# An adaLN attention and ternary feed-forward kernel on one core: weight preparation of the first attention spread anew over VectorE, GpSimd and ScalarE

## The chip, the core and the metric

The kernel runs on one core of a Trainium2 chip. The metric is the device time of one execution in microseconds (us). Engines are named as in the profile: PE is TensorE, PEld its weight load, DVE is VectorE, ACT is ScalarE, POOL is GpSimd, SP is SyncE, whose queue issues DMAs. PSUM banks have the names QA, QB, T, F0, F1, SA, SB, PV; the profile prints F0 and F1 both as F.

## What is computed

For each of 16 sequences of 256 tokens and 512 features, an adaptive RMS norm, an attention of 16 heads, an output projection, and a feed-forward part with ternary weights; the input is added at the end.

```python
xn = rms_norm(x, g_norm) * (1.0 + scale) + shift          # scale, shift = emb @ W_emb + b_emb
q, k, v = split(xn @ W_qkv)                               # 16 heads of 32
q, k = rms_norm(q, g_q), rms_norm(k, g_k)
o = softmax(q @ k.T * 32 ** -0.5) @ v
y = o + o @ W_out
def ternarize_weights(w):
    gamma = mean(abs(w))
    return sign(round(w / (gamma + EPS))) * gamma
h = gelu(bitlinear(y, w_fc))                              # bitlinear: layer norm, then x_hat @ ternary(w).T
x = x + bitlinear(h, w_proj)                              # w_fc 2048x512, w_proj 512x2048
```

## The kernel before

The kernel is written engine by engine; the order of each engine's instructions is fixed by hand, and semaphores tie the engines together. It runs as a pipeline over sequences: `iteration(i)` works on up to five sequences at once (`late` = i-2 second feed-forward half, `ffn` = i-1, `att` = i, `qkv` = i+1, `pre` = i+2). Each iteration has a front part (maxima of the logits, layer norm, eight feed-forward units) and then a loop `for h in range(HEADS)` over the 16 heads of `att`, in which all other work is placed by tables from head number to step.

Iteration 0 is the first with attention. No feed-forward part runs in it. In its place the weights of both feed-forward matrices are made ternary and W_out's low half is made, all between the head steps. It is the only iteration that the change touches. Its head loop runs from about 57 us to about 102 us of the trace.

One head step `h` is, on each engine:

- PE: `scores(h)` into bank SA or SB (line 892; F0 and F1 for heads 2 and 3; it waits for `p_lo` of head h-2, in heads 4 and 5 of head h-4), then the fillers (pieces of the next sequence's q, k, v projection, lines 760 to 762), then `values(h-2)` into PV (lines 907 to 909), then `column_sums(c)` where the table `COLSUM_AT` has one (line 754, waits for `s_sign`), then one use of the bank T: a `heads` transpose (line 917) or a `piece` transpose of `qkn` (line 1068). `values` of the first head of each group of four waits for `o_sb` of the group before.
- ACT: exponential (line 1209), its f16 copy `p_hi` (line 1215), then a `Square` of a finished piece (line 1227), the high half of the transposed piece or heads (lines 1251, 1280), and last a sign pass of 2048 columns where `SIGN_AT` has one (line 1126).
- DVE: in heads 5, 9 and 13 first `heads_out` (lines 1408, 1410: reads PV, writes `o_sb`), then `p_lo` (line 1557), then the low halves, sums of squares `ssq` (line 1579), `qkn` (line 1583, waits for POOL's `rqk`), and last `out_weights_lo` (line 1341), `fc_cut` (lines 1330 and 1332, a pair) and `dve_round` (line 1318).
- POOL: only the power -0.5 for `rx` (line 672) and `rqk` (line 710), each when its `ssq` has come.

The weights of one ternary matrix are four blocks of 128x2048. A block (w, k), w 0 for w_fc and 1 for w_proj, goes through these steps: rounding (multiply by `inv`, add MAGIC, in place, f32), then either ACT's sign pass or DVE's `fc_cut` into f16. ACT's sign of block (1, 0) and (1, 1) also waits for `s_fcut` 1, that of (1, 2) and (1, 3) for `s_fcut` 2, since their destination lies over the raw blocks that `fc_cut` reads. PE's `column_sums(c)` waits for the sign of (1, c).

POOL rounds blocks (0, 2), (0, 3), (0, 0) ahead of iteration 0, right behind the scaling of W_out's high half (lines 655 and 660). DVE rounds (0, 1) and all four of w_proj in the head loop. The tables that the change touches, as they stand before:

```python
WO_LOW_AT, G_K_AT = 2, 3
DVE_ROUND_AT = {1: (0, 1), 4: (1, 0), 6: (1, 1), 9: (1, 2), 10: (1, 3)}
POOL_ROUNDS = (2, 3, 0)
FC_CUT_AT = {3: 0, 5: 1}
SIGN_AT = {6: (1, 0), 8: (1, 1), 10: (1, 2), 12: (1, 3)}
COLSUM_AT = {8: 0, 10: 1, 12: 2, 14: 3}
```

At the end of iteration 0, PE transposes piece 3 (line 1068), then the last heads (line 917). With that the front part of iteration 1 starts (line 760 into SA), and SP issues the 16 `stk` transfers.

Of the kernel before, what the change touches and what calls it, by code (L numbers as in the profile page):

```python
# [9 lines left out]
ALU = mybir.AluOpType  # L10
# [62 lines left out]
FIRST_V_AT = 9  # L73
SECOND_FILLER = {2: QKV[0][0:2], 3: QKV[0][2:4], 4: QKV[1][0:2], 5: QKV[1][2:4], 6: QKV[2][0:2], 7: QKV[2][2:4],
                 9: QKV[3][0:2], 10: QKV[3][2:4], 12: V[0][0:2], 14: V[0][2:3], 15: V[0][3:4] + V[1][0:1]}
SECOND_SQUARE_AT, SECOND_NORM_AT = {3: 0, 5: 1, 8: 2, 11: 3}, {4: 0, 7: 1, 10: 2, 13: 3}
SECOND_TURN_AT = {6: ("heads", 0), 7: ("piece", 0), 9: ("piece", 1), 10: ("heads", 1), 12: ("piece", 2),
                  14: ("heads", 2), 15: ("piece", 3)}
FIRST_SQUARE_AT, FIRST_NORM_AT = {0: 0, 1: 1, 3: 2, 5: 3}, {2: 0, 4: 1, 6: 2, 9: 3}
# [11 lines left out]
               10: [("q", n) for n in range(6, 8)]}  # L91
SUMS_AFTER_LOW = 3

SCALE_AT, SECOND_SCALE_AT = {1: (0,), 2: (1,), 3: (2,), 4: (3,)}, {12: (0, 1), 13: (2, 3)}

MAGIC = 1.5 * 2.0 ** 23
WO_LOW_AT, G_K_AT = 2, 3
FC_ABS_AT = {1: 0, 3: 1, 5: 2, 7: 3}
PROJ_ABS_AT, PROJ_ABS_ORDER = {12: 0, 14: 1}, (0, 1, 3, 2)
DVE_ROUND_AT = {1: (0, 1), 4: (1, 0), 6: (1, 1), 9: (1, 2), 10: (1, 3)}  # L100
DVE_ROUNDS = [DVE_ROUND_AT[h] for h in sorted(DVE_ROUND_AT)]
POOL_ROUNDS = (2, 3, 0)
FC_CUT_AT = {3: 0, 5: 1}
SIGN_AT = {6: (1, 0), 8: (1, 1), 10: (1, 2), 12: (1, 3)}
SIGNS = [(0, 2), (0, 3)] + [SIGN_AT[h] for h in sorted(SIGN_AT)]
WQ_LOW_UNIT, WQ_LOW_AT = {0: (0, 0, KT), 2: (1, 0, KT // 2)}, {1: (1, KT // 2, KT), 2: (2, 0, KT)}
WQ_LOW_DONE = (1, 3, 4)
COLSUM_AT = {8: 0, 10: 1, 12: 2, 14: 3}


def place(h):
# [27 lines left out]
def first(b):  # L139

    return isinstance(b, int) and b == 0
# [20 lines left out]
def early(b):  # L162

    return isinstance(b, int) and b < 1
# [19 lines left out]
def rms_at(i):  # L184

    return FIRST_RMS_AT if i == -1 else SECOND_RMS_AT if i == 0 else None
# [43 lines left out]
def adaln_ffn_kernel(nc, x, xT, condT, w_emb, b_emb, g_norm, g_qk, w_qkv, w_out, w_fcT, w_projT, out):  # L230
    with ExitStack() as ctx:  # L231
        def sb(name, shape, dt=F32):
            return ctx.enter_context(nc.sbuf_tensor(name, shape, dt))
# [4 lines left out]
        def sem(name):  # L238
            return ctx.enter_context(nc.semaphore(name))
# [26 lines left out]
        inv = sb("inv", [P, 2])  # L266
# [67 lines left out]
        ffn_raw = [[proj_raw[:, 0:F], proj_raw[:, F:2 * F], hs_raw[:, F:2 * F], hg_raw[:, 0:F]],  # L334
                   [hq_raw[:, 0:F], hq_raw[:, F:2 * F], hs_raw[:, 0:F], hg_raw[:, F:2 * F]]]
# [297 lines left out]
        def _(pool):  # L633
# [13 lines left out]
            def first_weights():  # L647
# [10 lines left out]
                pool.wait_ge(s_abs, 4)  # L658
                for k in POOL_ROUNDS:
                    pool.tensor_scalar(ffn_raw[0][k], ffn_raw[0][k], inv[:, 0:1], MAGIC, ALU.mult, ALU.add  # L660
                                       ).then_inc(fc_round, 1)

            def iteration(i):
# [17 lines left out]
                def add_q(n):  # L681
                    pool.wait_ge(hsq_r, nth(ffn, UNITS, n + 1))
                    if n > 1:
                        pool.wait_ge(sumq_r, nth(ffn, UNITS - 1, n - 1))
                    pool.tensor_tensor(acc[:, 1, :], hq[:, 0, :] if n == 1 else acc[:, 1, :], hq[:, n, :], ALU.add  # L685
                                       ).then_inc(sumq_r, 1)

                if pre is not None and not early(pre) and rms_at(i) is None:
                    rms(pre)
                if ffn is not None:  # L690
# [29 lines left out]
        def _(pe):  # L720
# [85 lines left out]
            def iteration(i):  # L806
# [230 lines left out]
                for h in range(HEADS):  # L1037
# [21 lines left out]
                    if isinstance(i, int) and i == -1 and h == FIRST_V_AT:  # L1059
                        weight_sums(0)  # L1060
                    if isinstance(i, int) and i == 0 and h in COLSUM_AT:
                        column_sums(COLSUM_AT[h])
                    kind, n = turn_at(i).get(h, (None, 0))
# [39 lines left out]
        def _(act):  # L1103
# [14 lines left out]
            def signs(w, k):  # L1118

                if (w, k) in DVE_ROUNDS:  # L1120
                    act.wait_ge(s_dround, DVE_ROUNDS.index((w, k)) + 1)
                else:
                    act.wait_ge(fc_round, POOL_ROUNDS.index(k) + 1)
                if w:
                    act.wait_ge(s_fcut, k // 2 + 1)
                act.activation(ternary_rows(w, k), ffn_raw[w][k], ACT.Sign, bias=unmagic[:, 0:1]).then_inc(s_sign, 1)
# [20 lines left out]
            def iteration(i):  # L1147
# [57 lines left out]
                for h in range(HEADS):  # L1205
# [81 lines left out]
        def _(dve):  # L1287
# [33 lines left out]
            def fc_cut(k):  # L1321

                dst = ternary_rows(0, k)
                if k == 0:
                    dve.wait_ge(wo_h, 2)
                if k == 0:
                    dve.wait_ge(fc_round, POOL_ROUNDS.index(0) + 1)
                else:
                    dve.wait_ge(s_dround, DVE_ROUNDS.index((0, 1)) + 1)
                dve.tensor_scalar(dst, ffn_raw[0][k], MAGIC, 1.0, ALU.subtract, ALU.min).then_inc(s_cut, 1)  # L1330
                dve.wait_ge(s_cut, k + 1)
                dve.tensor_scalar(dst, dst, -1.0, None, ALU.max).then_inc(s_fcut, 1)
# [148 lines left out]
            def iteration(i):  # L1481
# [67 lines left out]
                for h in range(HEADS):  # L1549
# [87 lines left out]
                    if isinstance(i, int) and i == 0 and h == WO_LOW_AT:  # L1637
                        out_weights_lo()
                    if isinstance(i, int) and i == 0 and h in FC_CUT_AT:
                        fc_cut(FC_CUT_AT[h])  # L1640
                    if isinstance(i, int) and i == 0 and h in DVE_ROUND_AT:
                        dve_round(*DVE_ROUND_AT[h])
                    if isinstance(i, int) and i == 0 and h == HEADS - 1:
# [51 lines left out]
```

## Time and profile before

| | |
|---|---|
| device time, median of 3 runs | 1096.38 us (1095.32 to 1097.99) |
| the profiled execution | 1096.41 us, of which the span of the trace is 1094.5 us |
| busy share of the span | PE 96%, PEld 61%, DVE 83%, ACT 73%, POOL 50% |
| head loop of iteration 0 | about 57 to 102 us |

The profile is one execution with a start and a duration for every instruction. From 120 us on the PE is busy in nearly every slice of the profile; the only stretches with gaps on the PE are the first 120 us and the last few. The trace is read here through the order in time of one engine's instructions, the waits, and the busy time of each engine in a stretch.

### The profile page before, as it was taken

Reading aid. Unit: us, or ns where it says so; the run is one execution under the profiler, and the core shown is the slowest. Engines: PE = TensorE matmul, PEld = TensorE weight load, DVE = VectorE, ACT = ScalarE, POOL = GpSimd, SP = SyncE. Lnnn points to the kernel's source line nnn. Section 1 sums busy time; section 2 is a strip of 40 time slices with the busy share of each in tenths; the row PEclk is TensorE's granted clock in tenths of the full one; section 3 lists DMA queues with packets and bytes.
Section 4 is the critical chain, followed back from the end, with each engine's and each line's share of the span. In section 5 each row is a group of like instructions: output and inputs, shape, how many; then the busy total and the mean of one; then the engine's idle time right before and its main releaser. Section 6 shows DMA issues by size and latency. Waiting matters only on the chain. (4 is left out here: it accounts for less than half of the span.)

```text
span 1094.5 us, 24406 instructions
## 1 busy us (share of the span) xinstructions
PE 1053.1 (96%) x9457; PEld 666.7 (61%) x9457; DVE 910.9 (83%) x1630; ACT 802.6 (73%) x1371; POOL 550.2 (50%) x367
## 2 busy tenths in 40 slices
PE   8668899999999999999999999999999999999898
PEld 2334666656666665666666566666656566665656
DVE  4787788888898988889898888889889898868667
ACT  4876786858688685868868586786858688584854
POOL 1932471917447191744719174471917447191613
PEclk9899899999999999999999999999999999999999
DMA  9922204131221413222041312214131220212100
GB/s 349 323 51 43 79 3 97 45 78 64 45 67 32 97 45 78 64 47 68 30 96 45 78 64 48 68 30 95 45 78 64 48 68 29 59 40 59 59 20 21
DMA packets 79698, 77.13 MB, mean 70 GB/s; under 512 B 8656, under 2 KB 60256, under 8 KB 79072
## 3 DMA queue, kind: packets, MB, share of 16 engines
q1 hardware_dynamic: 79552, 75.58, 25.1%
q8 instruction: 75, 1.23, 0.5%
q14 instruction: 39, 0.32, 0.1%
q10 hardware_dynamic: 32, 0.01, 0.0%
HBM read 41.85 MB, written 8.40 MB: 46 GB/s over the span
## 5 line engine op out<-in xcount | busy, mean ns | idle before, releaser
L987 PE MATMUL F<-yT_hi,fc_t 128*128 128x256 f16 (+1 forms) x1040 | 228.5, 272 | 1.1 <-DVE yT_lo L1399 1.1
L988 PE MATMUL F<-yT_lo,fc_t 128*128 128x256 f16 (+1 forms) x1040 | 228.2, 272 | 0.0
L710 POOL TENSOR_TENSOR rqk<-ssq,half 128x16 f32<-128x16 f32 x64 | 197.4, 3091 | 40.8 <-DVE ssq L1579 40.8
L830 PE MATMUL F<-proj_t,hs 128*128 128x512 f16 (+1 forms) x512 | 192.3, 377 | 0.0
L832 PE MATMUL F<-proj_t,hs 128*128 128x512 f16 (+1 forms) x512 | 191.8, 376 | 0.0
L1540 DVE SCALAR_TENSOR_TENSOR hs<-hg,g_inv,hs 128x512 f16<-128x512 f32 x128 | 145.3, 1143 | 31.3 <-ACT hs L1198 31.1
L678 POOL TENSOR_TENSOR acc<-acc,hg 128x512 f32<-128x512 f32 x96 | 147.2, 1533 | 14.5 <-ACT hg L1193 1.5
L685 POOL TENSOR_TENSOR acc<-acc,hq 128x512 f32<-128x512 f32 x90 | 114.3, 1270 | 13.9 <-ACT hq L1267 5.2
L1193 ACT ACTIVATE hg<-F,g_fc 128x512 f32<-128x512 f32 x128 | 87.3, 682 | 43.3 <-PE F L988 43.2
L672 POOL TENSOR_TENSOR rx<-msx,half 128x2 f32<-128x2 f32 x16 | 12.2, 763 | 203.2 <-DVE msx L1293 188.3
L987 PEld LDWEIGHTS F<-yT_hi,fc_t 128*128 128x128 f16 x1040 | 102.1, 98 | 20.0 <-issue 6.5
L668 POOL TENSOR_TENSOR rs<-var,half 128x1 f32<-128x1 f32 x32 | 17.7, 552 | 190.4 <-DVE var L1388 190.4
L907 PEld LDWEIGHTS PV<-v_hi,p_hi 128*128 128x128 f16 x1024 | 88.2, 96 | 36.4 <-issue 12.1
L988 PEld LDWEIGHTS F<-yT_lo,fc_t 128*128 128x128 f16 x1040 | 102.2, 98 | 11.5
L907 PE MATMUL PV<-v_hi,p_hi 128*128 128x33 f16 x1024 | 104.5, 178 | 3.8 <-DVE o_sb L1410 3.7
L1557 DVE TENSOR_TENSOR p_lo<-SA,p_hi 128x512 f16<-128x512 f32 x123 | 84.6, 688 | 25.3 <-ACT p_hi L1215 24.6
L909 PE MATMUL PV<-v_hi,p_lo 128*128 128x33 f16 x1024 | 103.6, 177 | 0.0
L908 PE MATMUL PV<-v_lo,p_hi 128*128 128x32 f16 x1024 | 103.4, 177 | 0.0
L1557 DVE TENSOR_TENSOR p_lo<-SB,p_hi 128x512 f16<-128x512 f32 x123 | 84.4, 686 | 19.0 <-ACT p_hi L1215 15.8
L908 PEld LDWEIGHTS PV<-v_lo,p_hi 128*128 128x128 f16 x1024 | 83.5, 96 | 24.6 <-issue 0.6
L1198 ACT ACTIVATE hs<-hg,g_inv 128x512 f16<-128x512 f32 x128 | 92.4, 722 | 4.2
L1209 ACT ACTIVATE SA<-SA 128x512 f32<-128x512 f32 x123 | 72.4, 589 | 16.3 <-PE SA L892 15.6
(260 smaller groups left out, 2741.2 us busy)
## 6 DMA issues: line engine op xcount, KB each, us to landing
stk<-qkT SPq DMA_DIRECT2D x128, 128.0 KB, 2.5
xtok<-in_x SPq DMA_DIRECT2D x17, 512.0 KB, 3.8
xT_sb<-in_xT SPq DMA_DIRECT2D x16, 512.0 KB, 3.5
stk<-qkT SPq DMA_DIRECT2D x128, 64.0 KB, 2.2
xres<-in_x SPq DMA_DIRECT2D x15, 512.0 KB, 3.7
out<-xres SPq DMA_DIRECT2D x15, 512.0 KB, 2.8
stk<-in_w_emb SPq DMA_DIRECT2D x4, 512.0 KB, 6.9
fc_t<-in_w_qkv SPq DMA_DIRECT2D x2, 1024.0 KB, 11.0
```

What stands on the lines that cost most here:

```text
L678: pool.tensor_tensor(acc[:, 0, :], hg[:, 0, :] if n == 1 else acc[:, 0, :], hg[:, n, :], ALU.add).then_inc(sumh_r, 1)
L685: pool.tensor_tensor(acc[:, 1, :], hq[:, 0, :] if n == 1 else acc[:, 1, :], hq[:, n, :], ALU.add).then_inc(sumq_r, 1)
L710: pool.tensor_tensor(rqk[:, n % 2, :], ssq[:, n % 2, :], half[:, :], ALU.pow).then_inc(rqk_r, 1)
L830: pe.matmul(dst, hs[:, 0, k // 2, col:col + P], proj_t[:, k, cols], start=(k == 0), stop=False)
L832: mm = pe.matmul(dst, hs[:, 1, k // 2, col:col + P], proj_t[:, k, cols], start=False, stop=(k == FT - 1))
L907: pe.matmul(dst, ph, v_hi[:, k, h, :], start=(k == 0), stop=False)
L908: pe.matmul(dst[:, 0:DH], ph, v_lo[:, k, h, :], start=False, stop=False)
L909: mm = pe.matmul(dst, p_lo[:, h % (BEHIND + 1), k, t * P:(t + 1) * P], v_hi[:, k, h, :], start=False, stop=(k == TT - 1))
L987: pe.matmul(dst, w, yT_hi[:, k, cols], start=(k == 0), stop=False)
L988: mm = pe.matmul(dst, w, yT_lo[:, k, cols], start=False, stop=(k == KT - 1))
L1540: dve.scalar_tensor_tensor(hs[:, 1, n, :], hg[:, n, :], g_inv[:, 0:1], hs[:, 0, n, :], ALU.mult, ALU.subtract).then_inc(hlo_r, 1)
L1557: dve.tensor_tensor(p_lo[:, h % (BEHIND + 1), :, :], score_bank(att, h)[:, :].rearrange("p (k n) -> p k n", k=TT), p_hi[:, h % (BEHIND + 1 ...
```

## The change

It moves three roundings of DVE to POOL: block (0, 1) becomes the last of the roundings ahead of iteration 0, and blocks (1, 0) and (1, 1) are rounded by POOL at the start of iteration 0, behind a wait for W_out's low half. `out_weights_lo` on DVE goes from head 2 to head 0. The two `fc_cut` go from heads 3 and 5 to heads 4 and 6, the two roundings that stay on DVE from heads 9 and 10 to heads 8 and 9, `qkn` of piece 0 from head 4 to head 5, and the four `scale_input` from heads 12 and 13 to heads 11 and 14. The signs on ACT go from heads 6, 8, 10, 12 to 5, 6, 9, 11, and the column sums on PE from heads 8, 10, 12, 14 to 7, 8, 11, 13. Nothing computed is changed.

```diff
-SECOND_SQUARE_AT, SECOND_NORM_AT = {3: 0, 5: 1, 8: 2, 11: 3}, {4: 0, 7: 1, 10: 2, 13: 3}
+SECOND_SQUARE_AT, SECOND_NORM_AT = {3: 0, 5: 1, 8: 2, 11: 3}, {5: 0, 7: 1, 10: 2, 13: 3}
...
-SCALE_AT, SECOND_SCALE_AT = {1: (0,), 2: (1,), 3: (2,), 4: (3,)}, {12: (0, 1), 13: (2, 3)}
+SCALE_AT, SECOND_SCALE_AT = {1: (0,), 2: (1,), 3: (2,), 4: (3,)}, {11: (0, 1), 14: (2, 3)}
...
-WO_LOW_AT, G_K_AT = 2, 3
+WO_LOW_AT, G_K_AT = 0, 3
...
-DVE_ROUND_AT = {1: (0, 1), 4: (1, 0), 6: (1, 1), 9: (1, 2), 10: (1, 3)}
+DVE_ROUND_AT = {8: (1, 2), 9: (1, 3)}
 DVE_ROUNDS = [DVE_ROUND_AT[h] for h in sorted(DVE_ROUND_AT)]
-POOL_ROUNDS = (2, 3, 0)
-FC_CUT_AT = {3: 0, 5: 1}
-SIGN_AT = {6: (1, 0), 8: (1, 1), 10: (1, 2), 12: (1, 3)}
+POOL_ROUNDS = (2, 3, 0, 1)
+POOL_PROJ_ROUNDS = (0, 1)
+FC_CUT_AT = {4: 0, 6: 1}
+SIGN_AT = {5: (1, 0), 6: (1, 1), 9: (1, 2), 11: (1, 3)}
...
-COLSUM_AT = {8: 0, 10: 1, 12: 2, 14: 3}
+COLSUM_AT = {7: 0, 8: 1, 11: 2, 13: 3}
...
+                if isinstance(i, int) and i == 0:
+                    pool.wait_ge(wo_h, 2)
+                    pool.wait_ge(s_thr, 4)
+                    pool.wait_ge(s_abs, 8)
+                    for k in POOL_PROJ_ROUNDS:
+                        pool.tensor_scalar(ffn_raw[1][k], ffn_raw[1][k], inv[:, 1:2], MAGIC, ALU.mult, ALU.add
+                                           ).then_inc(proj_round, 1)
...
                 if (w, k) in DVE_ROUNDS:
                     act.wait_ge(s_dround, DVE_ROUNDS.index((w, k)) + 1)
+                elif w:
+                    act.wait_ge(proj_round, POOL_PROJ_ROUNDS.index(k) + 1)
...
-                if k == 0:
-                    dve.wait_ge(fc_round, POOL_ROUNDS.index(0) + 1)
-                else:
-                    dve.wait_ge(s_dround, DVE_ROUNDS.index((0, 1)) + 1)
+                dve.wait_ge(fc_round, POOL_ROUNDS.index(k) + 1)
```

## Rows read from the trace of the kernel before

**Rows 1.** Busy time of each engine in two stretches; columns as the first line says.
```profile
core 0: us, PE busy (x) PEld busy (x) DVE busy (x) ACT busy (x) POOL busy (x), PEclk, DMA share, GB/s
...
57.00:104.00 47.00, 35.22 (x349) 19.75 (x346) 38.55 (x65) 35.38 (x59) 14.17 (x5) 0.96 0.12 27
...
60.00:65.00 5.00, 4.67 (x38) 2.30 (x39) 3.98 (x5) 4.41 (x11) 0.00 (x0) 0.68 0.33 108
```

**Rows 2.** Waits from 57 to 104 us: in total, times, longest.
```profile
DVE p_lo L1557 <- ACT p_hi L1215: 5.0, 7, 1.2
ACT oT_hi L1280 <- PE T L917: 4.6, 3, 3.1
```

**Rows 3.** PE in order of time: start us, us, instruction [idle before <-releaser].
```profile
69.86 0.39 PE L892 MATMUL SA<-stk 97*128 97x256 f16 x2 [1.25 <-DVE p_lo L1557]
...
73.88 0.18 PE L907 MATMUL PV<-v_hi,p_hi 128*128 128x33 f16 x1 [2.33 <-DVE o_sb L1410]
...
98.08 0.63 PE L1068 MATMUL T<-ident,qkn 128*128 128x128 f32 x4 [0.42 <-DVE oT_lo L1416]
...
101.44 0.44 PE L917 MATMUL T<-ident,o_sb 128*128 128x128 f32 x2 [0.18 <-DVE o_sb L1410]
```

**Rows 4.** Groups of DVE instructions, 56 to 104 us: count, busy us, mean ns, idle before.
```profile
L1318 DVE TENSOR_SCALAR hq<-hq,inv 128x2048 f32<-128x2048 f32 x2 | 2.6, 1278 | 0.0
L1330 DVE TENSOR_SCALAR fc_t<-proj_t 128x2048 f16<-128x2048 f32 x2 | 2.4, 1218 | 0.0
L1341 DVE SCALAR_TENSOR_TENSOR wo_lo<-fc_t,wo_hi 128x2048 f16<-128x2048 f32 x1 | 2.3, 2281 | 0.0
```

**Rows 5.** DVE in order of time in iteration 0.
```profile
54.33 1.67 DVE L1479 SCALAR_TENSOR_TENSOR xT_sb<-xT_sb,cur_a,rx_all 128x256 f32<-128x256 f32 x4 [0.55 <-DMA rx_all<-rx_row]
...
58.00 0.69 DVE L1557 TENSOR_TENSOR p_lo<-SA,p_hi 128x512 f16<-128x512 f32 x1 [0.98 <-ACT p_hi L1215]
...
69.12 0.68 DVE L1557 TENSOR_TENSOR p_lo<-SA,p_hi 128x512 f16<-128x512 f32 x1
71.28 0.69 DVE L1583 TENSOR_TENSOR qkn<-QA,rqk 128x512 f32<-128x512 f32 x1 [1.47 <-POOL rqk L710]
...
76.72 0.68 DVE L1557 TENSOR_TENSOR p_lo<-SA,p_hi 128x512 f16<-128x512 f32 x1
```

**Rows 6.** ACT in order of time in iteration 0.
```profile
65.92 0.60 ACT L1215 ACTIVATE p_hi<-SA 128x512 f16<-128x512 f32 x1
...
68.36 0.60 ACT L1227 ACTIVATE sq<-QB 128x512 f32<-128x512 f32 x1
70.30 0.58 ACT L1209 ACTIVATE SA<-SA 128x512 f32<-128x512 f32 x1 [1.33 <-PE SA L892]
...
74.92 2.00 ACT L1126 ACTIVATE proj_t<-hq,unmagic 128x2048 f16<-128x2048 f32 x1
76.81 0.59 ACT L1209 ACTIVATE SB<-SB 128x512 f32<-128x512 f32 x1
...
79.04 0.59 ACT L1209 ACTIVATE SA<-SA 128x512 f32<-128x512 f32 x1
...
80.22 0.59 ACT L1227 ACTIVATE sq<-F 128x512 f32<-128x512 f32 x1
```

**Rows 7.** POOL in order of time, before and in iteration 0.
```profile
42.14 5.37 POOL L655 TENSOR_SCALAR wo_hi<-fc_t 128x2048 f16<-128x2048 f32 x1
...
51.51 1.98 POOL L660 TENSOR_SCALAR proj_t<-proj_t,inv 128x2048 f32<-128x2048 f32 x1
...
67.53 3.71 POOL L710 TENSOR_TENSOR rqk<-ssq,half 128x16 f32<-128x16 f32 x1
...
82.01 2.90 POOL L710 TENSOR_TENSOR rqk<-ssq,half 128x16 f32<-128x16 f32 x1 [3.03 <-DVE ssq L1579]
```

**Rows 8.** One scale_input of a late iteration and the POOL sums beside it.
```profile
909.49 5.50 POOL L685 TENSOR_TENSOR acc<-acc,hq 128x512 f32<-128x512 f32 x4
910.01 1.02 DVE L1479 SCALAR_TENSOR_TENSOR xT_sb<-xT_sb,cur_a,rx_all 128x256 f32<-128x256 f32 x1
```

More of the change, by code:

```diff
@@ L378, in adaln_ffn_kernel @@
         fc_round = sem("fc_round")
+        proj_round = sem("proj_round")
         wo_i = sem("wo_i")
```

## The prediction, made blind

> **What bounds the kernel now.** The page's slices come first: behind 120 us the PE is busy nearly without a gap, so a change in iteration 0 is worth what it moves the start of iteration 1, and that shift is carried to the end. Then the busy time of the stretch: of 47 us the PE works 35.2, DVE 38.6, ACT 35.4, POOL 14.2 [rows 1]. No engine fills it, so it is read through its waits. DVE waits for ACT's p_hi (5.0 us), ACT for the heads transpose on PE (4.6) [rows 2], PE for p_lo and o_sb of DVE [rows 3]. It is a ring in which each engine queues behind the long passes of another. The worst knot lies at 66 to 77 us. p_hi of head 4 ends at 65.92+0.60 = 66.52 [rows 6], but its p_lo comes at 69.12, behind out_weights_lo, ssq and the cut on DVE [rows 5]. scores(6) waits for it until 69.86 [rows 3], so the exponential of head 6 starts at 70.30 after 1.33 idle [rows 6]. Then DVE waits 1.47 for rqk, does qkn and a rounding, and only then heads_out, for which PE waits 2.33 [rows 3, 5]; ACT waits 3.1 for the transpose behind that [rows 2]. I follow the ring head by head, first up to p_lo of head 6 (76.72 before, [rows 5]), then along ACT, then to the last two transposes of the iteration, at 98.08 and 101.44 [rows 3].
>
> **Unit costs.** From start to start: exponential and p_hi of a head 80.22-79.04 = 1.18 on ACT; a sign 76.81-74.92 = 1.89 [rows 6]. The heads' high half takes ACT some 0.3, a square 0.5, a piece's high half 0.5 to 0.6. On DVE a p_lo, ssq, qkn or piece's low half takes 0.60 (its busy time less the 0.09 that overlap), a rounding 1.20, out_weights_lo 2.20, a cut 1.25 and its second pass 0.6, together 1.85 [rows 4, 5]. A rounding on POOL is 1.98 [rows 7]. A consumer starts 0.03 to 0.06 behind what it waits for.
>
> **Ahead of the loop.** The rounding of (0,1) on POOL follows at 53.46 and ends at 55.44 (51.51+1.95, +1.98) [rows 7]. It runs beside the four scale_input of DVE at 54.33 [rows 5]; before, POOL stood idle there. The nearest rows have one scale_input at 1.02 beside POOL's sums instead of the 1.67/4 = 0.42 that it takes alone [rows 5, 8]. Bounds: nothing, or DVE standing still to 55.44, which is 1.11. DVE idles 0.98 before p_lo of head 0 [rows 5], so 0 to 0.15 reaches the loop; I take 0.15. The Trainium skill, "Perfetto Trace Analysis", section Optimizing Scalar/DVE Operations, says that offloading between the two engines might not help, as they share a read port of SBUF. Rows 8 show such a collision. By that rule alone the sum would lose its POOL part; in this kernel only this one round meets DVE passes with two SBUF inputs, and the cover of 0.98 hides it.
>
> **out_weights_lo to head 0.** It runs from 60.21 to 62.49, so p_lo of head 1 slips by 1.7 to 62.42. Its readers on PE, values(1) and scores(5), stand behind four and more passes of the q, k, v projection, which hold PE to 64.5: it costs nothing. p_lo of head 3 then comes right behind its p_hi, at 64.4. ssq 0 follows at 65.4, p_lo of head 4 at 66.55 instead of 69.12.
>
> **The roundings on POOL.** Released at 62.5, they end at 64.5 and 66.5 (2 x 1.95). rx and rqk queue behind them: rx to 67.2, rqk 0 takes 2.90 alone and 3.71 beside the two-pass cut [rows 7], so it ends between 70.1 and 71.1; I take 71.0, since fc_cut 0 now runs at 67.15 to 69.09, beside it. qkn 0, which stands one head later, has its turn on DVE at 70.8: it waits 0.2 instead of 1.47. What queues behind it is p_lo of head 6, which isn't due before 72.36.
>
> **Up to head 6.** scores(6) starts right behind values(3) at 68.5 instead of 69.86. heads_out 0 comes at 69.0, o_sb is there at 69.65, values(4) starts at 70.0 instead of 73.88. But ACT now has the sign of (1,0) in front of exponential 6. It is free at 68.36+0.50 = 68.86 and waits for fc_cut 0 until 69.15. So exponential 6 starts at 71.04, 0.7 later than before, p_hi 6 ends at 72.33, and p_lo 6 starts at 72.36 instead of 76.72: **4.4 us early**.
>
> **From there ACT is the bound.** Its work from 69.15 to the end of head 15 is 4 signs x 1.89 = 7.6, 10 heads x 1.18 = 11.8, three heads' high halves 0.8, three pieces' 1.6, two squares 1.0: 22.8. It is fed in time except twice. The high half of piece 1 waits 0.4 (norm 1 at 76.3 to 76.9, two thirds of piece 3 on PE to 78.3, values(7), the transpose to 79.28), and the sign of (1,2) 0.15 for the rounding that DVE does at 78.7 to 80.0. That is 23.3, and the last p_hi is issued by 92.4. On PE that releases scores(15) at 90.8, the rest of V with values(13) to 92.6, and then the transpose of piece 3: 92.6 against 98.08, 5.5 early. The four scale_input (0.8 each pair) fall into DVE's waits or 0.45 before p_lo 15, which isn't due before values(15) at 94.0. From that transpose to the last one the order is as before, piece halves, colsum, heads_out: 101.44-98.08 = 3.36 [rows 3]. So 95.96 instead of 101.44.
>
> **The sum.** 5.5 - 0.15 = 5.3 us. Only 3 x 1.20 = 3.6 of it is work taken from DVE; the rest are waits that the knot no longer makes. SP's transfers wait for the piece's low half and move with it; the column sums and signs are all done by then. The profiled execution took 1096.4 and the median is 1096.38, so the forecast is 1096.4 - 5.3 = **1091.1**. Hand-kept lists of this sort drop small waits, some 0.1 at each of a dozen handovers, so 4.0 to 6.0 is its own range: 1090.4 to 1092.4.
>
> **Rivals.**
>
> A. *The knot is only moved.* DVE's idle time stays as it is, and the gain is only the removed work, 3.6, less the wait that the early sign makes at exponential 6 (0.7) and a late rqk (up to 0.9): 2.0 to 3.6, 1092.8 to 1094.4. For it: the sign in head 5 holds six later exponentials in one queue, and ACT has no slack left behind it. Against: the idle time of DVE at rqk (1.47) and of PE at o_sb (2.33) has a cause that goes away. Chance 0.22.
>
> B. *The two engines get in each other's way*, so that POOL's rounds cost DVE what they save: each of the three stops DVE for its length or is stopped. Three times 1.95 lost on DVE (5.9) against 3.6 saved and some 2 to 3 of resolved waits gives 0 to 1 gained, 1095.4 to 1096.4. The Trainium skill, "GPSIMD Engine Reference", section Specifications, lists contention with DVE instructions in a 2-port mode or with two SBUF inputs. Against it: from 62.5 to 66.5 DVE has p_lo and ssq, which read one SBUF tensor each, unlike the pass in rows 8. Chance 0.07.
>
> C. *POOL becomes the bound: slower.* If a rounding took as long as the pass at 42.14, also 128x2048, 5.37 [rows 7], the two would end at 73.3, rqk 0 at 76.9, and qkn 0 with p_lo 6 behind it would come at 77.0 and 77.6, 0.9 later than 76.72. Of the forecast's gain only what is won behind head 6 is left (1.1). Then it is about even, and slower once the two take 0.2 more than this; with 1 us more each, and rqk lengthened again, it is 1098 to 1100. Against it: in rows 7 a rounding into f32 takes 1.98; the 5.37 is a pass into f16. Chance of the case 0.05, of a loss over 0.3% 0.03.
>
> D. *The clock of PE.* At 60 to 65 us it is granted 0.68 on average [rows 1]: the first passes behind PE's wait for the input's low half run at the lower level, 1.2 GHz. A new such stretch would cost some 1.5 to 2 us, which is what six passes at half rate lose (6 x 0.21 = 1.3). The new order has shorter gaps (1.0 at most, against 2.33 [rows 3]), so I see none: gain 3.3 to 4. Chance 0.06.
>
> The change does what it says: the same passes run on another engine, and the order is written out, so nothing else moves.
>
> **How the numbers follow.** Forecast 0.60; A 0.22; B 0.07; C 0.05; D 0.06. About 0.3%, 3.3 us, is what a measurement can tell from no change. Faster by more than that, under 1093.1: the forecast 0.60, D 0.05, and of A the part with 3.3 or more, 0.05: 0.70. Slower by more: 0.03. Within it: 0.27. Range: the cases reach from the forecast's 1090.4 to C's 1100. With a fifth of the chance left out, A and D are in, B and C out, so it ends at 1094.8, the 0.4 over A's end being part of what three runs spread; on the low side it takes the forecast's end less such a spread, 1.1: 1089.3.
>
> **What would show it.** p_lo of head 4 right behind its p_hi near 66.6; POOL with two passes of 1.98 from 62.5; qkn of piece 0 waiting under 0.5; no 2.3 us gap on PE before values(4); a sign on ACT at 69.1, and from there to the last head hardly an idle time on ACT; the last transpose (line 917) of iteration 0 near 96. The forecast is wrong if ACT idles over 2 us between 69 and 92, if rqk 0 ends behind 72.4, or if the shift at the last transpose isn't found again at the end of the trace.

## The result and the profile after

| | before | after |
|---|---|---|
| device time, median | 1095.93 us (1094.49 to 1097.99) | 1090.86 us (1089.44 to 1091.40) |
| the profiled execution, its span | 1096.41 us, 1094.5 us | 1091.28 us, 1089.4 us |
| head loop of iteration 0: `p_lo` of head 0 to last transpose | 58.00 to 101.44 us: 43.44 | 57.37 to 96.66 us: 39.29 |

The ratio of after to before is 0.9944, with a 95% interval from 0.9932 to 0.9956: 0.56% faster, 5.1 us by the medians. I forecast 1091.1.

The span is 5.1 us shorter. The last transpose of iteration 0 comes 4.78 earlier (96.66 against 101.44), and what follows it is 992.7 us long in after and 993.1 in before. So nearly the whole gain lies ahead of iteration 1, as predicted.

The mean granted clock differs a little from execution to execution of one and the same kernel, and the time with it: of the 19 executions of before timed beside two_moves, the eight at 0.983 took 1097.6 us on average, the three at 0.989 took 1095.5. The gain isn't that: four of the five executions of after were at 0.987 and took 1089.84 to 1091.40 us, and before at 0.987 averaged 1095.7 to 1096.1 on the three occasions of the experiments.

Busy time of each engine in two stretches of after; the first stretch answers to the first row of [rows 1], the second has the same limits as there.

```profile
core 0: us, PE busy (x) PEld busy (x) DVE busy (x) ACT busy (x) POOL busy (x), PEclk, DMA share, GB/s
57.00:98.50 41.50, 35.20 (x337) 19.41 (x337) 36.28 (x63) 34.31 (x57) 18.57 (x7) 0.92 0.11 22
60.00:65.00 5.00, 5.00 (x24) 2.01 (x23) 4.41 (x5) 3.54 (x9) 3.06 (x2) 0.50 0.36 108
```

PE is busy as long as in before (35.20 against 35.22), ACT nearly so. DVE lost only 2.3 us of busy time (38.55 to 36.28), though three roundings of 1.28 left it: something on DVE became longer. And the granted clock from 60 to 65 us is 0.50, where it was 0.68 [rows 1]: PE did 24 instructions there instead of 38.

The waits of after in the head loop (in total, times, longest), for [rows 2]:

```profile
DVE p_lo L1565 <- ACT p_hi L1226: 4.0, 6, 1.4
...
ACT sq L1238 <- PE QA L771: 1.6, 1, 1.6
...
ACT oT_hi L1291 <- PE T L926: 1.3, 1, 1.3
```

ACT waits 1.3 us for the heads transpose instead of 4.6, and the wait is one instead of three. In before, the multiplication `cur_s` ahead of the loop is

```profile
53.63 0.15 DVE L1463 TENSOR_SCALAR cur_s<-mod_s 128x4 f32<-128x4 f32 x1
```

DVE of after in order of time, from there to `p_lo` of head 6, for [rows 5]:

```profile
52.59 1.79 DVE L1471 TENSOR_SCALAR cur_s<-mod_s 128x4 f32<-128x4 f32 x1
54.65 1.67 DVE L1487 SCALAR_TENSOR_TENSOR xT_sb<-xT_sb,cur_a,rx_all 128x256 f32<-128x256 f32 x4 [0.26 <-DMA rx_all<-rx_row]
...
59.56 2.28 DVE L1349 SCALAR_TENSOR_TENSOR wo_lo<-fc_t,wo_hi 128x2048 f16<-128x2048 f32 x1
...
64.33 1.54 DVE L1304 TENSOR_SCALAR msx<-ssx 128x2 f32<-128x2 f32 x1
...
67.17 0.69 DVE L1565 TENSOR_TENSOR p_lo<-SA,p_hi 128x512 f16<-128x512 f32 x1 [0.49 <-ACT p_hi L1226]
67.77 1.22 DVE L1338 TENSOR_SCALAR fc_t<-proj_t 128x2048 f16<-128x2048 f32 x1
...
71.42 0.68 DVE L1591 TENSOR_TENSOR qkn<-QA,rqk 128x512 f32<-128x512 f32 x1
...
73.02 0.69 DVE L1565 TENSOR_TENSOR p_lo<-SA,p_hi 128x512 f16<-128x512 f32 x1 [0.93 <-ACT p_hi L1226]
```

`p_lo` of head 4 now waits for its `p_hi` instead of standing behind other work, `qkn` waits for nothing, and `p_lo` of head 6 is 15.65 us behind that of head 0, where it was 18.72. But the multiplication of a 128x2 tensor, `msx`, takes 1.54 us. POOL in order of time tells why (for [rows 7]):

```profile
50.44 3.92 POOL L662 TENSOR_SCALAR proj_t<-proj_t,inv 128x2048 f32<-128x2048 f32 x2
...
61.94 3.92 POOL L695 TENSOR_SCALAR hq<-hq,inv 128x2048 f32<-128x2048 f32 x2 [7.58 <-DVE wo_lo L1349]
...
66.75 3.01 POOL L719 TENSOR_TENSOR rqk<-ssq,half 128x16 f32<-128x16 f32 x1
```

The two roundings of w_proj end at 65.86, and `msx` ends at 65.87. The two ahead of the loop end at 54.36, and DVE's 128x4 `cur_s` at 54.38. Both tiny operations stand on DVE until the POOL pass that is running is over. The four `scale_input` behind `cur_s` start at 54.65 only when their DMA has landed, so that stand costs them nothing.

ACT behind that, for [rows 6]:

```profile
69.81 2.00 ACT L1137 ACTIVATE proj_t<-hq,unmagic 128x2048 f16<-128x2048 f32 x1 [0.24 <-DVE fc_t L1340]
...
71.72 0.58 ACT L1220 ACTIVATE SA<-SA 128x512 f32<-128x512 f32 x1
...
80.00 0.69 ACT L1262 ACTIVATE qkT<-T,g_k 128x512 f16<-128x512 f32 x1 [0.33 <-PE T L1077]
...
92.63 0.60 ACT L1226 ACTIVATE p_hi<-SB 128x512 f16<-128x512 f32 x1
```

From the sign of block (1,0) at 69.81 to the last `p_hi` at 92.63, the trace marks only these two waits on ACT, 0.57 us together, the first of them in front of the sign. PE, for [rows 3]:

```profile
59.70 0.61 PE L769 MATMUL QA<-wq_hi,xn_hi 128*128 128x512 f16 x1 [2.63 <-DVE xn_lo L1372]
...
64.28 0.63 PE L770 MATMUL QA<-wq_lo,xn_hi 128*128 128x512 f16 x1
64.71 0.60 PE L771 MATMUL QA<-wq_hi,xn_lo 128*128 128x512 f16 x1
...
93.28 0.64 PE L1077 MATMUL T<-ident,qkn 128*128 128x128 f32 x4
...
96.66 0.44 PE L926 MATMUL T<-ident,o_sb 128*128 128x128 f32 x2 [0.18 <-DVE o_sb L1418]
```

The first twelve passes of the q, k, v projection are 0.4 us apart, PE's lower level (1.2 GHz). PE of before at the first of them, the seventh (the first at the higher level) and the one behind the twelfth:

```profile
60.33 0.61 PE L760 MATMUL QA<-wq_hi,xn_hi 128*128 128x512 f16 x1 [2.95 <-DVE xn_lo L1364]
...
63.23 0.38 PE L760 MATMUL QA<-wq_hi,xn_hi 128*128 128x512 f16 x1
...
65.05 0.38 PE L760 MATMUL QB<-wq_hi,xn_hi 128*128 128x512 f16 x1
```

The same twelve passes there take 4.72 us to the next bank (65.05 less 60.33), and 5.96 in after (65.66 less 59.70).

### The profile page after: what moved, and what is told of

Its sections match the earlier page's. It is cut to its first block and busy times, and to the rows that moved or that the text cites. A ratio compares the mean times of both kernels' runs of the same rounds, so it can differ in the third digit from the quotient of the medians.

```text
span 1089.4 us, 24404 instructions
## 1 busy us (share of the span) xinstructions
PE 1053.6 (97%) x9457; PEld 666.6 (61%) x9457; DVE 910.4 (84%) x1627; ACT 802.1 (74%) x1371; POOL 556.3 (51%) x370
## 5 line engine op out<-in xcount | busy, mean ns | idle before, releaser
L1220 ACT ACTIVATE SA<-SA 128x512 f32<-128x512 f32 x123 | 72.4, 589 | 15.4 <-PE SA L901 14.6
```

## The experiments

In each, "the loop" is the time from the start of `p_lo` of head 0 to the start of the last heads transpose of iteration 0, in the profiled execution (before 43.44, after 39.29). What follows that transpose took 991.5 to 993.3 us in all 14 kernels, so the loop and where it begins carry the differences. The loop began between 57.3 and 58.8 us, without order, so its length is compared and not its end. Ratios are to before, timed on the same chip, with 95% intervals. Diffs are against after unless said otherwise.

### order_only: the order without POOL

All tables of the change, but the three roundings stay on DVE.

```diff
-DVE_ROUND_AT = {8: (1, 2), 9: (1, 3)}
+DVE_ROUND_AT = {1: (0, 1), 3: (1, 0), 5: (1, 1), 8: (1, 2), 9: (1, 3)}
...
-POOL_ROUNDS = (2, 3, 0, 1)
+POOL_ROUNDS = (2, 3, 0)
...
-                    for k in POOL_PROJ_ROUNDS:
-                        pool.tensor_scalar(ffn_raw[1][k], ffn_raw[1][k], inv[:, 1:2], MAGIC, ALU.mult, ALU.add
...
```

> The changed order, but all three roundings back on VectorE (in heads 1, 3 and 5). If the gain comes from the knot that the new order undoes, the 3.6 us of roundings fall mostly into VectorE's waits at 62 to 66 us and cost 0.6 to 1 us: 4.0 to 4.5 us faster than before, near 1091.8. If the gain is the work taken from VectorE, 1.5 us faster than before at most, near 1094.5.

Measured: 1091.50 us (1090.43 to 1093.84), ratio 0.9965 (0.9951 to 0.9978), loop 39.66. DVE in order of time:

```profile
64.84 0.16 DVE L1297 TENSOR_SCALAR msx<-ssx 128x2 f32<-128x2 f32 x1
...
66.26 1.28 DVE L1322 TENSOR_SCALAR hq<-hq,inv 128x2048 f32<-128x2048 f32 x1
67.45 0.68 DVE L1561 TENSOR_TENSOR p_lo<-SA,p_hi 128x512 f16<-128x512 f32 x1
...
72.30 1.28 DVE L1322 TENSOR_SCALAR hq<-hq,inv 128x2048 f32<-128x2048 f32 x1
73.49 0.68 DVE L1561 TENSOR_TENSOR p_lo<-SA,p_hi 128x512 f16<-128x512 f32 x1
```

Most of the gain is there with not one instruction taken from DVE: the loop is 3.8 of the 4.15 us shorter. The timed ratio has 0.35% of after's 0.56%, with intervals that overlap; the profiled execution was among the fastest of its five (1090.50, two others took 1093.8), so the loop shows this kernel at its better end. The rows show what hides the roundings. The one in head 3 takes the place of what `msx` loses to POOL in after (0.16 here, 1.54 there). The one in head 5 lies where DVE of after waits 0.93 us for `p_hi` of head 6, so `p_lo` of head 6 comes 16.04 behind that of head 0, against 15.65.

### pool_only: POOL without the order

The roundings on POOL as in the change, with its other tables as in before.

```diff
-SECOND_SQUARE_AT, SECOND_NORM_AT = {3: 0, 5: 1, 8: 2, 11: 3}, {5: 0, 7: 1, 10: 2, 13: 3}
+SECOND_SQUARE_AT, SECOND_NORM_AT = {3: 0, 5: 1, 8: 2, 11: 3}, {4: 0, 7: 1, 10: 2, 13: 3}
...
-WO_LOW_AT, G_K_AT = 0, 3
+WO_LOW_AT, G_K_AT = 2, 3
...
-FC_CUT_AT = {4: 0, 6: 1}
-SIGN_AT = {5: (1, 0), 6: (1, 1), 9: (1, 2), 11: (1, 3)}
+FC_CUT_AT = {3: 0, 5: 1}
+SIGN_AT = {6: (1, 0), 8: (1, 1), 10: (1, 2), 12: (1, 3)}
...
```

> The three roundings on GpSimd, but every table as before (W_out's low half in head 2, so GpSimd starts its two passes near 66 us). Knot: rx and rqk of piece 0 now stand behind 3.9 us of passes, which takes back what VectorE saves: 0 to 1.5 us faster than before, 1094.5 to 1096. Removed work: 3 to 3.6 us faster than before, near 1092.5.

Measured: 1098.31 us (1097.04 to 1100.62), ratio 1.0020 (1.0012 to 1.0029), loop 46.57. DVE, then POOL, in order of time:

```profile
66.32 1.57 DVE L1304 TENSOR_SCALAR msx<-ssx 128x2 f32<-128x2 f32 x1
67.80 0.69 DVE L1587 TENSOR_REDUCE ssq<-sq 128x16 f32<-128x528 f32 x1
68.41 2.49 DVE L1338 TENSOR_SCALAR fc_t<-proj_t 128x2048 f16<-128x2048 f32 x1
...
71.54 0.68 DVE L1565 TENSOR_TENSOR p_lo<-SA,p_hi 128x512 f16<-128x512 f32 x1
...
74.42 0.69 DVE L1591 TENSOR_TENSOR qkn<-QA,rqk 128x512 f32<-128x512 f32 x1 [2.20 <-POOL rqk L719]
```
```profile
65.90 3.92 POOL L695 TENSOR_SCALAR hq<-hq,inv 128x2048 f32<-128x2048 f32 x2 [12.19 <-DVE wo_lo L1349]
...
71.45 2.94 POOL L719 TENSOR_TENSOR rqk<-ssq,half 128x16 f32<-128x16 f32 x1
```

Three roundings less on DVE, and the kernel is slower than before; neither of my two cases had that. `msx` stands for 1.57 instead of 0.16, until POOL's first pass is over at 67.9, and the cut takes 2.49 instead of 1.22, since it stands until the second is over at 69.8. So `p_lo` of head 4 is 13.80 behind that of head 0, against 11.12; and `qkn` waits 2.20 for the `rqk` that stood behind the roundings, against 1.47 in before. Together that is some 3.4 us, and the loop is 3.1 longer. This is the mechanism of rival B with the queue of rival C behind it. The change escapes it because W_out's low half in head 0 lets POOL end by 65.86, ahead of the cut at 67.77. It is slower clear of noise, though by 0.20% and not by the 0.3% that my "slower" stood for.

### no_wo_wait: POOL's roundings at once

```diff
-                    pool.wait_ge(wo_h, 2)
```

> The changed kernel without GpSimd's wait for W_out's low half: its two roundings start near 57 us, beside VectorE's passes over two SBUF tensors (the input's low half, then W_out's). If the two engines shut each other out, the input's low half comes up to 2.9 us late and with it the first q, k, v piece: 1 to 3 us slower than the changed kernel. If they only share, under 0.5 us slower.

Measured: 1093.41 us (1092.96 to 1094.51), ratio 0.9976 (0.9968 to 0.9985), loop 42.10. POOL, then DVE:

```profile
57.17 4.08 POOL L694 TENSOR_SCALAR hq<-hq,inv 128x2048 f32<-128x2048 f32 x2 [2.52 <-DVE inv L1344]
```
```profile
57.92 4.40 DVE L1371 SCALAR_TENSOR_TENSOR xn_lo<-xT_sb,cur_s,xn_hi 128x256 f16<-128x256 f32 x4
```

The four `xn_lo` have two inputs in SBUF. Beside POOL's pass they take 4.40 us instead of 1.66, PE waits 4.80 for them instead of 2.63, and the loop is 2.8 longer. The wait for `wo_h`, which I had taken only as the time of release, is worth more than half of the gain: it keeps POOL's passes away from DVE's passes with two inputs.

### norm_head4 and norm5_only: where `qkn` of piece 0 stands

norm_head4 is after with `qkn` of piece 0 back in head 4. norm5_only is before with it in head 5, and nothing else.

```diff
-SECOND_SQUARE_AT, SECOND_NORM_AT = {3: 0, 5: 1, 8: 2, 11: 3}, {5: 0, 7: 1, 10: 2, 13: 3}
+SECOND_SQUARE_AT, SECOND_NORM_AT = {3: 0, 5: 1, 8: 2, 11: 3}, {4: 0, 7: 1, 10: 2, 13: 3}
```

> The changed kernel with qkn of piece 0 back in head 4, ahead of fc_cut 0. If VectorE's wait for GpSimd's rqk is what the later place avoids, VectorE stands still from 67.8 to 69.8 us, fc_cut 0 and the sign behind it come 2 to 2.6 us late: 2 to 2.6 us slower than the changed kernel. If the place doesn't matter because the time is bound by other work: within 0.5 us of it.

> The kernel before with one entry moved: qkn of piece 0 from head 4 to head 5. If VectorE's wait of 1.47 us for rqk and what queues behind it (heads_out 0, for which TensorE waits 2.3 us) is a part of the knot of its own, 1 to 1.8 us faster than before, near 1095. If the knot needs all the moves together, within 0.5 us of before.

Measured: norm_head4 1094.86 us, ratio 0.9984 (0.9975 to 0.9993), loop 41.72; norm5_only 1095.35 us, ratio 0.9988 (0.9980 to 0.9997), loop 41.76. DVE of norm_head4:

```profile
70.42 0.69 DVE L1591 TENSOR_TENSOR qkn<-QA,rqk 128x512 f32<-128x512 f32 x1 [1.86 <-POOL rqk L719]
```

One entry of a table makes 2.4 us of loop in after and 1.7 in before. `heads_out` stands behind `qkn` on DVE, and behind its `o_sb` stand `values` of head 4 on PE, so a wait of 1.86 for `rqk` stops three engines. In norm_head4 ACT waits 2.8 us for the cut and PE 2.2 for `o_sb`. The timed gain of norm5_only, 0.12% or 1.3 us, is near its 1.7 of loop, and not zero by its interval. By the medians norm_head4 loses 4.0 us against after; 2.4 of that is loop, and 0.8 its later beginning, which this entry doesn't touch.

### two_moves: how far two table entries carry

Before with `qkn` of piece 0 in head 5 and W_out's low half in head 0 (diff against before).

```diff
...
-WO_LOW_AT, G_K_AT = 2, 3
+WO_LOW_AT, G_K_AT = 0, 3
```

> The kernel before with two entries moved: qkn of piece 0 to head 5 and W_out's low half to head 0; all roundings, cuts and signs stay. With qkn alone the head loop took 41.8 us against 43.4. If W_out's low half in head 2 is the rest of the knot (it holds p_lo of heads 3 and 4 and ssq 0), the loop takes 40 to 41 us and the kernel is 3 to 3.5 us faster than before. If the places of the cuts matter as much, it stays near 41.8 us, 1.5 us faster than before.

Measured: 1093.88 us (1092.48 to 1095.87), ratio 0.9975 (0.9965 to 0.9985), loop 41.00. `p_lo` of head 4 comes at 67.98, 10.24 behind that of head 0. So the steps of the loop are: 43.44 before, 41.76 with `qkn` moved, 41.00 with W_out's low half too, 39.66 with the roundings, cuts, signs and scales reordered as well (order_only), 39.29 with POOL. The first step is larger than what the low stretch of the clock shifted between before and after (1.24). The third isn't the clock's either, which from 63 to 66 us was lower in order_only (0.77) than in two_moves (0.86). The second and fourth are within what it can shift. By the timed ratios before, two_moves and after are apart from each other; the single steps between neighbours behind norm5_only are not, since their intervals overlap.

### signs_late: is the early sign worth something?

```diff
-SIGN_AT = {5: (1, 0), 6: (1, 1), 9: (1, 2), 11: (1, 3)}
+SIGN_AT = {6: (1, 0), 8: (1, 1), 10: (1, 2), 12: (1, 3)}
...
-COLSUM_AT = {7: 0, 8: 1, 11: 2, 13: 3}
+COLSUM_AT = {8: 0, 10: 1, 12: 2, 14: 3}
```

> The changed kernel with the signs in heads 6, 8, 10, 12 and the column sums in 8, 10, 12, 14, as before. If ScalarE is the bound from 69 us on, its work is the same and only 0.5 to 1 us more of idle time arises at heads 6 and 7: 0 to 1 us slower than the changed kernel. If the early signs are what brings the gain, 2 to 4 us slower.

Measured: 1092.52 us (1090.32 to 1092.97), ratio 0.9955 (0.9943 to 0.9967), loop 38.94. `p_lo` of head 6 comes 14.02 behind that of head 0, 1.6 sooner than in after (the sign no longer stands in front of its exponential, and the clock was a little higher), and yet the loop is only 0.35 shorter. In this trace, then, the 0.7 us that I charged to exponential 6 for the sign in front of it is not lost: ACT has the same work to do until the last head. That is what an engine that bounds the stretch looks like. The times are less clear than the trace: the profiled execution was the fastest of the five, the other four took 1091.94 to 1092.97, and by the ratios this kernel is 0.1% slower than after with intervals that overlap. So a loss of 1 to 2 us by the late signs isn't excluded by the times, and isn't seen in the trace.

### pool_load: four more passes on POOL

After, with four spare passes of 128x2048 over a dead buffer right behind the two roundings.

```diff
+                    pool.wait_ge(s_sign, 2)
+                    for n in range(4):
+                        if n:
+                            pool.wait_ge(spare, n)
+                        pool.tensor_scalar(ffn_raw[0][3], ffn_raw[0][3], 1.0, 0.0, ALU.mult, ALU.add
+                                           ).then_inc(spare, 1)
```

> The changed kernel with four spare passes of 128x2048 on GpSimd (multiply by 1 in a buffer that is free) behind its two roundings, so that rx and rqk come 7.8 us later, rqk 0 near 77.5 us. Rival C of the prediction puts qkn 0 and p_lo of head 6 behind that: 4 to 6 us slower than the changed kernel, about even with before or up to 1 us slower. If GpSimd's place in the queue doesn't matter: within 0.5 us of the changed kernel.

Measured: 1098.51 us (1095.59 to 1100.06), ratio 1.0011 (1.0002 to 1.0019), loop 47.05, 7.8 more than after. POOL, then DVE:

```profile
66.60 9.02 POOL L702 TENSOR_SCALAR hg<-hg 128x2048 f32<-128x2048 f32 x4
```
```profile
68.63 2.94 DVE L1345 TENSOR_SCALAR fc_t<-proj_t 128x2048 f16<-128x2048 f32 x1
71.60 2.26 DVE L1347 TENSOR_SCALAR fc_t<-fc_t 128x2048 f16<-128x2048 f16 x1
...
79.22 0.69 DVE L1598 TENSOR_TENSOR qkn<-QA,rqk 128x512 f32<-128x512 f32 x1 [3.58 <-POOL rqk L726]
```

The 4 to 6 us that I expected came from the queue in front of `rqk` alone, and `p_lo` of head 6 does come 6.0 later behind that of head 0 than in after. A second stop comes on top: the two passes of the cut on DVE take 2.94 and 2.26 instead of 1.22 and 0.69, 3.3 us more, and ACT's sign waits for them:

```profile
73.96 2.00 ACT L1144 ACTIVATE proj_t<-hq,unmagic 128x2048 f16<-128x2048 f32 x1 [3.53 <-DVE fc_t L1347]
```

From there to the last `p_hi`, ACT's marked waits come to 8.1 us, 3.5 of them for the cut and the others for PE, where after had 0.57. That is nearly the whole loss of the loop. Rival C's mechanism exists, but here it took 9 us more of POOL passes to make the kernel slower than before; in after, `rqk` is there at 69.76, 1.66 ahead of its reader.

### after_busy and order_busy: the clock of PE

Ten matmuls without use, once, behind `scores` of heads 0 to 3, so that PE isn't idle before the first pass of the projection; in after and in order_only.

```diff
                                 for ahead in range(4):
                                     scores(ahead)
+                                keep_busy(PV, 10)
```

> The changed kernel with ten spare matmuls of 128x512 on TensorE behind the scores of heads 0 to 3, where it waits 2.6 us for the input's low half. If the low clock of the first q, k, v piece (12 passes at 0.43 us instead of 0.215) comes from that wait, the piece ends 2 us sooner; VectorE's mean_square, which stood 1.4 us beside GpSimd's rounding until 65.9 us, then limits what is left: 0.5 to 1.5 us faster than the changed kernel. If the clock doesn't follow: the same, or up to 2 us slower where the spare matmuls run at the low clock.

> The kernel with the changed order and all roundings on VectorE, with ten spare matmuls behind the scores of heads 0 to 3. There is no GpSimd pass at 62 to 66 us that could stop mean_square here. If that stop is what took the fast clock's gain in the changed kernel, this one gains more from the same matmuls: p_lo of head 4 at 9.0 to 9.4 us behind p_lo of head 0 instead of 10.0, VectorE's own rounding taking the rest, and a loop of 38.8 to 39.3 us against 39.7 without the matmuls.

Measured: after_busy 1091.83 us (1090.26 to 1093.10), ratio 0.9953 (0.9942 to 0.9965), loop 38.52; order_busy 1092.07 us (1090.92 to 1093.76), ratio 0.9957 (0.9944 to 0.9970), loop 38.92. The two stretches of after_busy, and its PE at the first pass of the projection:

```profile
57.00:98.50 41.50, 35.80 (x349) 19.79 (x349) 36.66 (x67) 34.37 (x58) 18.45 (x7) 1.00 0.11 27
60.00:65.00 5.00, 4.89 (x51) 2.73 (x52) 4.41 (x6) 4.84 (x11) 2.65 (x2) 1.00 0.32 108
```
```profile
60.11 0.39 PE L769 MATMUL QA<-wq_hi,xn_hi 128*128 128x512 f16 x1 [0.59 <-DVE xn_lo L1373]
```

With full clock the loop is 0.8 shorter than in after, and `p_lo` of head 4 comes 9.05 behind that of head 0, not 9.80. The total isn't shorter by what can be measured, against the 0.5 to 1.5 us that I expected. In order_busy `p_lo` of head 4 comes 9.26 behind that of head 0 instead of 10.00, the same 0.75 us sooner as in after_busy, so `msx` took nothing of the gain that shows. But the clock was granted at 0.50 from 56 to 60 us and 0.78 from 60 to 63, in spite of the same ten matmuls, so this is no sure remedy, and the two kernels can't be compared at equal clock.

Over all the kernels, the granted clock from 60 to 63 us was 0.50 in nine of the fourteen. From 63 to 66 it was 0.97 in before, 0.64 in after, 0.77 in order_only, 0.86 in two_moves and 0.50 in no_wo_wait. The four kernels with the ten matmuls had 0.76 or more from 60 to 63 us. Among the others I found no tie between the change and how long the low stretch lasts, and one profile each can't tell it from what differs between executions: the mean clock of before alone differs by enough for some 2 us between its own.

### busy_msx4: `msx` out of POOL's way

after_busy, with `msx` and `rx` one head later, behind POOL's roundings.

```diff
-FIRST_MSX_AT, SECOND_MSX_AT = 5, 3
+FIRST_MSX_AT, SECOND_MSX_AT = 5, 4
...
-FOLD_AT, SECOND_RMS_AT, RS2_AT, STAT_AT, OUT1_AT = 10, 3, 12, 14, 15
+FOLD_AT, SECOND_RMS_AT, RS2_AT, STAT_AT, OUT1_AT = 10, 4, 12, 14, 15
```

> The changed kernel with the ten spare matmuls, and with mean_square on VectorE and the power behind it on GpSimd in head 4 instead of head 3. If VectorE's small op waits out GpSimd's whole pass (1.56 us instead of 0.16), ssq 0 comes 1.3 us sooner, the cut and the first sign 1.0 us, and the head loop takes 37.5 us instead of 38.5. If the small op was merely last in line for something else: no change, 38.5.

Measured: 1090.37 us (1088.52 to 1091.46), ratio 0.9938 (0.9927 to 0.9950), loop 38.34. `msx` takes 0.16 us again (at 67.19), and `p_lo` of head 4 comes 8.78 behind that of head 0. The stop is gone, but `ssq` now waits 0.54 for the square, since PE's clock was low again here (0.50 from 56 to 60 us, 0.76 from 60 to 63). I had expected a loop of 37.5 us. The kernel has the fastest median of all, but its interval overlaps that of after, so this kernel isn't shown to be faster.

### dve_cut: ACT's fourth sign to DVE

busy_msx4, with all roundings of w_proj on POOL, and block (1,3) cut by DVE in head 12 instead of by ACT's sign, to take 1.89 us from the engine that bounds the stretch.

```diff
-DVE_ROUND_AT = {8: (1, 2), 9: (1, 3)}
+DVE_ROUND_AT = {}
...
-SIGN_AT = {5: (1, 0), 6: (1, 1), 9: (1, 2), 11: (1, 3)}
+SIGN_AT = {5: (1, 0), 6: (1, 1), 9: (1, 2)}
...
+                    if isinstance(i, int) and i == 0 and h == 6:
+                        for k in POOL_PROJ_ROUNDS[2:4]:
+                            pool.tensor_scalar(ffn_raw[1][k], ffn_raw[1][k], inv[:, 1:2], MAGIC, ALU.mult, ALU.add
...
+                    if isinstance(i, int) and i == 0 and h == 12:
+                        last_cut()
```

> As the one before, and the last two roundings on GpSimd as well (behind rqk 1, near 75 us), and block (1, 3) made ternary by VectorE in head 12 instead of by ScalarE's sign in head 11. If ScalarE's work is the bound from 69 us on, taking 1.9 of 22.8 us from it gives 1 to 1.8 us of loop, less what VectorE's 1.85 us for the cut costs where it is late: 36 to 37 us. If VectorE is the bound: no gain, or a loss up to 0.5 us.

Measured: 1095.51 us (1092.01 to 1099.37), ratio 0.9986 (0.9974 to 0.9999), loop 43.32, 5.0 more than busy_msx4. DVE, then PE and ACT:

```profile
73.94 2.35 DVE L1348 TENSOR_SCALAR fc_t<-fc_t 128x2048 f16<-128x2048 f16 x1
...
88.81 1.22 DVE L1354 TENSOR_SCALAR proj_t<-hg 128x2048 f16<-128x2048 f32 x1
90.06 0.69 DVE L1356 TENSOR_SCALAR proj_t<-proj_t 128x2048 f16<-128x2048 f16 x1
```
```profile
90.81 1.89 PE L770 MATMUL F<-proj_t,ones 128*128 128x512 f16 x4 [2.76 <-DVE proj_t L1356]
92.50 0.64 PE L908 MATMUL SA<-stk 97*128 97x256 f16 x2
92.92 0.63 PE L776 MATMUL QA<-wq_hi,xn_hi 128*128 128x512 f16 x1
```
```profile
93.17 0.58 ACT L1228 ACTIVATE SA<-SA 128x512 f32<-128x512 f32 x1 [3.81 <-PE SA L908]
```

`p_lo` of head 6 came 13.94 behind that of head 0, earlier than in any other kernel. Then the new cut, last in DVE's step, held the column sums of block 3, and behind them `scores` of head 14 stood in PE's queue: PE idle for 2.76 us, ACT for 3.81, and the passes behind that gap at the lower level (0.63 us each). The second pass of the other cut was stopped by one of the new POOL roundings (2.35 instead of 0.69). I had expected a loop of 36 to 37 us. Taking work from the engine that bounds a stretch won nothing here; the rows put that down to the place of the cut, in front of PE's column sums and `scores`, but no run has it elsewhere.

## Why the prediction came true, step by step

**The total and the place.** 1091.1 forecast, 1090.86 measured. "A change in iteration 0 is worth what it moves the start of iteration 1": the part behind the last transpose is 992.7 against 993.1 us. Of the signs that were to show the forecast wrong none came: ACT idled 0.57 us and not 2, `rqk` 0 ended at 69.76 and not behind 72.4, and the shift of 4.78 at the last transpose is found again at the end.

**Ahead of the loop: near in size, by luck.** I placed the rounding of (0,1) beside the four `scale_input` and took 0.15. The sum overlooked `cur_s`: in before it stands at 53.63, inside the 53.46 to 55.44 that I gave the rounding. In after it stood for 1.79 us until the pass was over at 54.36, and that pass no longer met `scale_input`. They began 0.32 later than in before, held by their DMA and not by DVE, and the loop began 0.63 earlier, within the scatter of its beginning over the kernels. Nothing of a cost can be seen.

**W_out's low half in head 0 "costs nothing": right, and too modest.** two_moves shows 0.8 of loop for it, though within what the clock scatters. Its greater worth is probably that it frees POOL early: pool_only has it two heads later and is slower than before. That kernel differs from after in the rest of the order too, so the share of this one entry isn't shown.

**POOL's roundings: the duration right, the company wrong.** Two passes took 3.92, as 2 x 1.95 said. "From 62.5 to 66.5 DVE has `p_lo` and `ssq`" forgot `msx`, a multiplication of 128x2 that took 0.16 and that I had left out for its size. It stood 1.4 us until the pass was over. In after that was hidden, since `ssq` needs the square of ACT, which waited 1.65 for PE and ended at 65.94, later than `msx`. `rqk` ended at 69.76 instead of 71.0, and `qkn` waited 0. About half of the 1.24 is that the power took 3.01 us although both passes of the cut ran inside it; the 3.71 of [rows 7], which I put down to the cut, isn't what such company always costs.

**The clock, rival D: partly happened, and I had seen none of it.** It isn't a new stretch behind a new gap. The stretch that was there lasted six passes longer: 12 passes take 5.96 us, against 4.72 in before: 1.24 more, near the 1.3 that the product of rival D gives for six passes, and less than the 1.5 to 2 that it charged. "The new order has shorter gaps" looked at the wrong gap: the wait for the input's low half stayed, 2.63 against 2.95. after_busy, at full clock, gets 0.8 of it back.

**Up to head 6: the knot did come loose, later than forecast.** By the sum, `p_lo` of head 6 would be 14.36 behind that of head 0 (72.36 less 58.00; the 0.15 ahead of the loop isn't in it). It was 15.65, against 18.72. The difference is there already at head 4, forecast 8.55 behind head 0 (66.55 less 58.00) and measured 9.80. The 1.29 too much are about what the six slow passes cost ahead of the square, 1.24. The sum had put that term at nothing. The 2.33 us that PE waited before `values` of head 4 are gone, as predicted.

**From there ACT is the bound: right, to the tenth with some luck.** From exponential 6 to the transpose of piece 3 I had 21.56 (92.6 less 71.04), and it took 21.56 (93.28 less 71.72). ACT's marked waits in it were 0.33, where the sum had 0.55, so its work took 0.2 more than added up and the two cancelled. From that transpose to the last one it took 3.38, against 3.36. The trace of signs_late agrees from the other side.

**So errors cancelled.** In the loop, 37.96 us was forecast (95.96 less 58.00) and 39.29 measured: 5.48 of gain against 4.15, 1.3 too much. The loop beginning 0.63 earlier, where I had it 0.15 later, and 0.3 us behind the last transpose made up for 1.1 us of it; neither comes from the change as far as the runs show. The forecast 5.3 and the measured 5.1 agree better than their parts do, and that is luck.

**Rival A fell, and with it a sentence of mine.** "Only 3 x 1.20 = 3.6 of it is work taken from DVE; the rest are waits" divides the gain wrongly, as A did. order_only takes no work away and shortens the loop by 3.8 of 4.15; pool_only takes all three away and makes it 3.1 longer. The removed work is worth some 0.4 of loop in this order (39.66 to 39.29, and with the ten matmuls 38.92 to 38.52, at unequal clock), and no more, since on DVE the roundings fall into its waits: it waits 2.5 us for `p_hi` in order_only and 4.0 in after, and one rounding takes the time that `msx` stands in after. Whether the timed difference between order_only (0.9965) and after (0.9944) is more than scatter is open: their intervals overlap, and they were timed on different occasions.

**Rival B was right as a mechanism.** Its own sum, 3.6 and 2 to 3 less 5.9, gives -0.3 to 0.7 and not 0 to 1, and I gave it the wrong victims. Not `p_lo` and `ssq`, but `msx`, `cur_s`, the cuts and `xn_lo`: in pool_only and no_wo_wait it costs 1.3 to 2.7 us a time. The Trainium skill, "SBUF — State Buffer", section Who interferes with whom, says that the pair of ports which VectorE and GpSimd share is an exclusive lock for a whole instruction, and that VectorE's `tensor_scalar` in its 2-port modes takes it too. By that, `msx` and the cuts should stop and `p_lo`, `ssq` not; the traces agree, with 1.54 for `msx`, 2.49 for a cut, and 0.67 to 0.70 for every single `p_lo` and `ssq`, beside a POOL pass or not.

## What to carry to other kernels

When a change moves work and reorders the rest at once, ask for each part what it would be worth alone: here the order alone gave nine tenths of what the loop won (six tenths of the timed gain, with intervals that overlap), and the move without the order was a loss. Before placing a long GpSimd pass, list every VectorE instruction that can run beside it, the tiny ones too: `msx` and `cur_s` waited for the end of the pass like the long cuts. Once an engine has no idle time left in a stretch, its work can be added up as a forecast: 21.6 us here, right within 0.2 in each part. Where it still waits for others, the clock of TensorE made the sum too good.

## What the runs showed of the hardware that I hadn't expected

- A VectorE `tensor_scalar` of 128x2 or 128x4 in f32 took 1.54 and 1.79 us beside a GpSimd pass over 128x2048, and 0.16 and 0.15 alone. It ended within 0.02 us of that pass.
- GpSimd's passes lengthened little where they came first: 3.92 for two beside VectorE's work, 4.08 in no_wo_wait beside the `xn_lo` that took 4.40 instead of 1.66. In dve_cut, where a rounding began inside a cut and the next cut pass inside that rounding, the two roundings took 2.55 and 2.40 instead of 1.98, and the four spare passes of pool_load took 9.02 instead of 7.8.
- GpSimd's power on 128x16 took 2.90 to 4.19 us in the head loops: 2.90 in pool_load while VectorE stood still, 3.01 in after with both passes of a cut inside it, 3.88 in order_only beside a rounding and a cut, 4.19 in after beside two roundings. What decides isn't shown.
- The granted clock of PE behind a wait of 2.6 to 2.95 us was 0.50 for six passes in before and for twelve in after, with the same instructions. In dve_cut it fell again behind the new gap of 2.76 us.
